# Second attention of a two-layer transformer kernel: two pairs on the two 64-row halves of the TensorE array, blocks of 16 score units, and row maxima moved by DMA

## What is computed

```python
Q = x @ wq + bq
K = x @ wk + bk
V = x @ wv + bv
Q = Q.reshape(B * H, S, D)      # B 4, H 16, S 1024, D 16: a plain reshape
K = K.reshape(B * H, S, D)
V = V.reshape(B * H, S, D)
scores = jnp.einsum('bqd,bkd->bqk', Q, K) / jnp.sqrt(jnp.float32(D))
attn = jax.nn.softmax(scores, axis=-1)
ctx = jnp.einsum('bqk,bkd->bqd', attn, V)
out = ctx.reshape(B, S, E) @ wo + bo + x      # and a layer norm
```

## Time and profile before

| | |
|---|---|
| median of 3 runs | 3050.78 us (3047.48 to 3051.34) |
| profiled execution, first to last instruction (span) | 3044.3 us |
| its own time | shown only as this span; what lies around it is in the runs' times |
| mean granted clock of TensorE | 0.896 |
| busy: PE / PE weight loads / DVE / ACT / POOL | 82% / 53% / 56% / 34% / 20% |

### The profile page before, as it was taken

How to read it: one execution, slowest core, us unless ns; L and a number is a source line. 1 busy time by engine, 2 the same in 40 slices (tenths; PEclk the granted TensorE clock), 3 DMA queues, 4 the chain that set the end, 5 groups by cost and what they waited for, 6 DMA issues and landing times. The chain is left out here.

```text
span 3044.3 us, 48668 instructions
## 1 busy us (share of the span) xinstructions
PE 2508.6 (82%) x15530; PEld 1604.6 (53%) x15531; DVE 1692.8 (56%) x2646; ACT 1020.5 (34%) x1877; POOL 602.4 (20%) x493
## 2 busy tenths in 40 slices
PE   3999999744889999999796859999999999945151
PEld 2777777642765555555585725545455455415041
DVE  3776777540333333333464457777777777537852
ACT  2444444210220000000222306666666666632010
POOL 4122121017000000000244311111111111120034
PEclk9999999756899999999898959999999999975566
DMA  5000000234421111110334893456364464011034
GB/s 194 2 0 0 0 0 0 83 141 171 160 83 33 34 36 35 34 34 31 118 114 144 241 114 28 29 39 46 29 46 39 35 50 28 1 59 56 0 105 144
DMA packets 213482, 193.01 MB, mean 63 GB/s; under 512 B 112810, under 2 KB 189266, under 8 KB 211314
## 3 DMA queue, kind: packets, MB, share of 16 engines
q1 hardware_dynamic: 198386, 140.07, 25.8%
q0 software_dynamic: 12672, 34.62, 3.7%
q10 hardware_dynamic: 2304, 16.78, 1.5%
HBM read 109.62 MB, written 81.79 MB: 63 GB/s over the span
## 5 line engine op out<-in xcount | busy, mean ns | idle before, releaser
L1621 DVE TENSOR_REDUCE a_nmax<-banks 128x1 f32<-128x1024 f32 x512 | 602.3, 1218 | 184.2 <-PE banks L1703 184.0
L1678 ACT ACTIVATE ga_probT<-banks 128x512 f32<-128x512 f32 x1024 | 555.9, 595 | 353.8 <-PE banks L1733 350.9
L1733 PE MATMUL banks<-a_qs,a_ks 128*128 128x512 f32 x1024 | 370.8, 439 | 17.9 <-ACT ga_probT L1678 8.7
L1703 PE MATMUL banks<-a_ks,a_qs 96*128 96x512 f32 x1024 | 309.8, 422 | 37.1 <-DMA ga_wo<-in_L_attn_wo_dram 27.4
L1654 POOL TENSOR_TENSOR a_qs<-ga_max_rows,a_tile_rows 32x1024 fp32r<-32x1024 f32 x64 | 151.4, 2365 | 758.7 <-DVE ga_max_rows L1627 758.7
L1733 PEld LDWEIGHTS banks<-a_qs,a_ks 128*128 128x128 f32 x1024 | 180.2, 193 | 210.3 <-ACT ga_probT L1678 178.7
L1179 PE MATMUL banks<-m_w,rb_xT 128*128 x576 | 288.9, 624 | 0.0
L1746 PE MATMUL banks<-ga_probT,a_v 128*32 128x512 f32 x2048 | 274.6, 608 | 0.9 <-ACT ga_probT L1678 0.9
L1026 PE MATMUL banks<-sh_xnT,sh_w 128*128 128x512 f32 x768 | 194.4, 409 | 81.0 <-issue 29.3
L1703 PEld LDWEIGHTS banks<-a_ks,a_qs 96*128 96x128 f32 x1024 | 192.0, 198 | 114.7 <-DVE a_nmax L1621 34.4
L1161 ACT ACTIVATE rb_silu<-banks 128x512 f32<-128x512 f32 x72 | 43.0, 597 | 516.1 <-PE banks L1179 516.1
(11 more groups left out here) (295 smaller groups left out, 3639.5 us busy)
## 6 DMA issues: line engine op xcount, KB each, us to landing
sh_xnT<-xnT_parts ACTq DMA_DIRECT2D x16, 1024.0 KB, 4.8
sorted_rows<-wa_zero SPq DMA_DIRECT2D x1, 9216.0 KB, 28.9
rb_xb<-sorted_rows POOLq DMA_DIRECT2D x72, 128.0 KB, 2.3
sorted_out<-rb_yb SPq DMA_DIRECT2D x72, 128.0 KB, 1.7
xnT_parts<-np_parts SPq DMA_DIRECT2D x8, 1024.0 KB, 4.5
m_w<-in_L_ffn_rw_dram SPq DMA_DIRECT2D x2, 4096.0 KB
values<-pg_v SPq DMA_DIRECT2D x16, 512.0 KB, 2.7
a_qs<-queries_rounded SPq DMA_DIRECT2D x32, 256.0 KB, 8.2
```

The costliest lines, as they stand in the source:

```text
L1621: nc.vector.tensor_reduce(nmax[:, gr, ST + q:ST + q + 1], slot[:], axis=AX.X, op=ALU.max, negate=True).then_inc(use_read, 1)
L1678: nc.scalar.activation(probT[(NS * pc + k) % SETS][n][:], b_t[h % 2][:], ACT.Exp, scale=SCALE).then_inc(exp_ready, 1)
L1703: last = nc.tensor.matmul(slot[:, HALF * hf:HALF * (hf + 1)], qs[a][0:ST, gr, P * q:P * (q + 1)], ks[a][0:ST, gr, HALF * hf:HALF * (hf + 1 ...
L1733: nc.tensor.matmul(b_t[h % 2][:], ks[a][:, n, P * k:P * (k + 1)], qs[a][:, n, HALF * hf:HALF * (hf + 1)], start=True, stop=True).then_inc( ...
```

## The change

Two pairs form a super, and there are eight. A pair's stacks now take 48 rows without gaps (three parts of 16), at row 0 for the first pair and at row 64 for the second; row 48 of each half is the row for the maxima in Q, with ones in K. Score products run over 48 rows, transposed ones over 49, each on a 64-row half of the array. A block is 16 score units: two pairs in turn, two groups, half of the queries. In a step PE issues a score product on one half, a transposed product of a block before on the other, and the same once more; the back half lags 22 units. The transposed products have three banks instead of two, `b_o` one instead of two, so that outputs are copied per block. Maxima are transposed once a block, and four DMAs from POOL write them to the rows at 48 and 112. The Fori loops of `group_attention` are gone: its steps are written out. `project_groups` loads the first super instead of the first pair, after waiting for both pairs' stores, and has fewer memsets.

```diff
+QK_IN, V_IN = 16 * 12, 16 * 2
+def load_super(eng, c, q_stack, k_stack, v, parts, values, qk_in, v_in):
+    for h in range(2):
+        for tile, n, blocks in ((q_stack, 0, (0, 0, 1)), (k_stack, 1, (0, 1, 0))):
+            for b, part in enumerate(blocks):
+                at = HR * h + DH * b
+                src = parts[n][part][2 * c + h].rearrange("(c d) (n t) -> d n c t", d=DH, n=NG)
+                eng.dma_start(tile[at:at + DH].bitcast(F32).rearrange("p n (c t) -> p n c t", c=PC), src).then_inc(qk_in, 16)
+        eng.dma_start(v[:, h].rearrange("p n q r -> p (n q r)"), values[2 * c + h]).then_inc(v_in, 16)
...
-            sp.wait_ge(parts_out[0], ONE + PARTS)
-            sp.wait_ge(v_out[0], ONE + 16)
-            load_pair(sp, 0, qs[0], ks[0], v_first, parts, values, first_in, first_in)
+            for s in range(2):
+                sp.wait_ge(parts_out[s], ONE + PARTS)
+                sp.wait_ge(v_out[s], ONE + 16)
+            load_super(sp, 0, qs[0], ks[0], v[0], parts, values, first_in, first_in)
...
-                nc.gpsimd.memset(ks[a][:].bitcast(F32), 0.0).then_inc(k_zero, 1)
...
-                nc.gpsimd.memset(qs[a][0:ST].bitcast(F32), 0.0).then_inc(stack_zero, 1)
...
+    HALF = L // 2
+    HQ = QT // 2
+    SUPERS = NP // 2
+    UB = 2 * 2 * HQ
+    BLOCKS = 4 * SUPERS
+    UNITS = UB * BLOCKS
+    LAG = UB + 6
+    SETS = 3
+    RING = 3
+    RB = UB // 2
...
+    def step_uses(s):
+        uses = [("scores", s)] if s < UNITS else []
+        if s % UB == 1 and UB < s < UNITS + UB:
+            uses.append(("maxima", s // UB - 1))
+        b, j = (s - LAG) // UB - 1, (s - LAG) % UB
+        if 0 <= b < BLOCKS and j == 3:
+            uses.append(("context", b))
+        if 0 <= b < BLOCKS and b % 2:
+            uses += [("contextT", b // 2)] * (j == 6) + [("project", b - 1)] * (j == 9) + [("project", b)] * (j == 11)
...
+            for b in range(BLOCKS):
...
+                pool.wait_ge(use_read, ONE + use_place["maxima", b] + 1)
+                for h in range(2):
+                    at = HR * h + ST
+                    for n in range(2):
+                        first = UB // 2 * h + HQ * n
+                        src = max_rows[b % 2][first:first + HQ].bitcast(F32)
+                        dst = q_cols[at:at + 1, 2 * gp + n].rearrange("o (q p) -> o q p", p=P)
+                        pool.dma_start(dst, src).then_inc(max_in[b % 2], 16)
...
+            def outputs(b):
+                act.wait_ge(pv_done, ONE + RB * (b + 1))
+                if b >= 2:
+                    act.wait_ge(use_done, ONE + use_place["context", b - 2] + 1)
+                nc.scalar.activation(o[b % 2][:], b_o[:], ACT.Copy).then_inc(o_ready, 1)
...
+            def scores(s, kh):
...
+                a, rows = c % SLOTS, slice(HR * h, HR * h + ST)
...
+            def scores_T(back, n):
...
+                a, h, kt = c % SLOTS, 1 - j % 2, j // 2
+                rows = slice(HR * h, HR * h + ST + 1)
+                if j == 0 and n == 0:
+                    pe.wait_ge(max_in[b % 2], 64 * (b // 2 + 1))
+                if w >= RING:
+                    pe.wait_ge(exp_ready, ONE + w - RING + 1)
+                nc.tensor.matmul(b_t[w % RING][:], ks[a][rows, 2 * gp + n, P * kt:P * (kt + 1)],
+                                 qs[a][rows, 2 * gp + n, HALF * hf:HALF * (hf + 1)], start=True, stop=True).then_inc(sT_done, 1)
...
+            for s in range(STEPS):
+                back = s - LAG
+                if s < UNITS:
...
+                    slot_of(use_place["scores", s])
+                    scores(s, 0)
+                if 0 <= back < UNITS:
+                    scores_T(back, 0)
+                if s < UNITS:
+                    scores(s, 1).then_inc(use_done, 1)
+                if 0 <= back < UNITS:
+                    scores_T(back, 1)
+                if back >= 2 and back % 2 == 0 and back <= UNITS:
+                    weigh(back // 2 - 1)
+                for kind, arg in step_uses(s):
+                    if kind != "scores":
+                        other[kind](arg)
```

More of the change, by code:

```diff
@@ L1506, in _, with group_attention @@
                 project(STEPS - 1, s)
[L1509 removed]
+def group_attention(nc, g, parts, values, qs, ks, v):
     ins = g.ins
[L1522 to L1555 removed]
@@ L1604, in _ @@
-            with sp.Fori(0, NP // SLOTS - 1) as r:
-                for c in range(SLOTS, 2 * SLOTS):
-                    load(r, c)
-            for c in range(NP // SLOTS * SLOTS, NP):
-                load(0, c)
+            for c in range(1, SUPERS):
+                a = c % SLOTS
+                if c >= SLOTS:
+                    sp.wait_ge(sT_done, ONE + 8 * UB * (c - SLOTS + 1))
+                    sp.wait_ge(pv_done, ONE + 4 * RB * (c - SLOTS + 1))
+                load_super(sp, c, qs[a], ks[a], v[a], parts, values, qk_in[a], v_in[a])
@@ L1687, in _, with weights @@
-            steps(act, step)
+            def weights(back, n):
+                w, k = 2 * back + n, back // 2
+                h = 1 - back % 2
+                act.wait_ge(sT_done, ONE + w + 1)
+                if back % 2 == 0 and n == 0 and k >= SETS:
+                    act.wait_ge(pv_done, ONE + k - SETS + 1)
+                nc.scalar.activation(probT[k % SETS][2 * h + n][:], b_t[w % RING][:], ACT.Exp, scale=SCALE).then_inc(exp_ready, 1)
+            def outputs(b):
[3 more added lines that the diff above has]
+                nc.scalar.activation(o[b % 2][:], b_o[:], ACT.Copy).then_inc(o_ready, 1)
@@ new lines, in maxima, with context @@
+            def maxima(b):
+                slot = slot_of(use_place["maxima", b])
+                pe.wait_ge(use_read, ONE + use_place["scores", UB * (b + 1) - 1] + 1)
+                nc.tensor.transpose(slot[:, 0:P], nmax[b % 2][:], g.ident[:]).then_inc(use_done, 1)
+            def context(b):
+                slot = slot_of(use_place["context", b])
+                pe.wait_ge(o_ready, ONE + b + 1)
+                for q in range(HQ):
+                    last = nc.tensor.transpose(slot[:, P * q:P * (q + 1)], o[b % 2][:, P * q:P * (q + 1)], g.ident[:])
+                last.then_inc(use_done, 1)
@@ new lines, in context_T, with project @@
+            def context_T(m):
+                slot = slot_of(use_place["contextT", m])
+                pe.wait_ge(use_read, ONE + use_place["context", 2 * m + 1] + 1)
+                for n in range(NG):
+                    last = nc.tensor.transpose(slot[:, P * n:P * (n + 1)], ctxn[:, n].rearrange("p q d -> p (q d)"), g.ident[:])
+                last.then_inc(use_done, 1)
+            def project(b):
+                slot = slot_of(use_place["project", b])
+                pe.wait_ge(use_read, ONE + use_place["contextT", b // 2] + 1)
+                h = b % 2
+                for a in range(A):
+                    last = nc.tensor.matmul(slot[:, 0:D], ctxT[:, h, a].rearrange("p n t -> p (n t)"), wo[:, a, :],
+                                            start=(a == 0), stop=(a == A - 1))
+                last.then_inc(use_done, 1)
@@ new lines, in _ @@
+            other = {"maxima": maxima, "context": context, "contextT": context_T, "project": project}
+            pe.wait_ge(w_in, ONE + 16 * QT)
+            for s in range(STEPS):
+                back = s - LAG
+                if s < UNITS:
+                    c = s // (4 * UB)
+                    if s % (4 * UB) == 0 and c > 0:
+                        pe.wait_ge(qk_in[c % SLOTS], ONE + QK_IN * (c // SLOTS + (c % SLOTS > 0)))
+                    slot_of(use_place["scores", s])
[8 more added lines that the diff above has]
+                    weigh(back // 2 - 1)
+                for kind, arg in step_uses(s):
+                    if kind != "scores":
+                        other[kind](arg)
```

311 lines of the change are left out of this document (99 added, 212 removed).

## The result

The changed kernel takes 3064.9 us (median of 12 runs, 3042.4 to 3078.6) against 3051.2 us for the kernel before, measured beside it (3034.8 to 3060.7): ratio 1.0039, 95% interval 1.0021 to 1.0057. It is slower by 0.4%. The forecast was 2935 us with a range of 2880 to 3046, so size and sign were wrong.

What follows compares the result with a forecast made beforehand. PE was taken to bound the kernel before, 98% busy in the joint stretch. Attention of 797 us plus 20 ahead, against 932.9, gave -116: span 2928, plus 6.5 for the runs' median, 2935 us; range 2880 to 3046.

Steps and rivals of the forecast that it cites:

- ahead of the attention: In project_groups, seven more loads on SP's queue before the last stores: 15 to 23 us, taken as 20.
- front: Start of the attention, only scores formed and reduced: 22 units at 1.378 us, 30.3 us.
- X: Time of one unit while both halves run: 1.712 us before, 1.48 forecast, own range 1.37 to 1.56.
- drain and tail: End of the attention after the last score product: 33 us for 22 units, plus 8.5 after the last weighing.
- Late by 0.55 us, taken as 0.6: Per block, PE's first transposed product waits for the maxima's POOL DMAs; bounds zero to some 5 us.
- twice the size at half the frequency and two supers of lead: no cost: Loads of the later supers during the attention were claimed to add no time.
- Maxima late: Rival: maxima DMAs land in 8 to 9 us instead of 4.75; 3055 us, or 2998 beside bursts only; chance 0.08.
- The clock: Rival: PE idling in the joint stretch brings 1.2 GHz, X 2.5; gain gone at a quarter of it; chance 0.04.
- The overlap of the halves: Score and transposed products on different row halves run at once, a pair in 0.233 us; chance 0.62.
- The loop through ACT: Products, two exponentials, then the weighing in PE's order: 2.71 us per two units, asking for X of 1.36.
- the rivals in which PE sets the pace: Own weights (3009 us, chance 0.12), no overlap (3046, 0.07), each change of half empties the array (3330, 0.07).
- Maxima and projections that stand in odd steps fall into its wait: In the joint stretch, this extra work was claimed to hide in the wait of ACT's loop.

Runs made afterwards that it cites:

- run 1: The changed kernel with the loads of supers 1 to 7 cut into small groups, each issued after a block's maxima have landed: 2891.05 us, ratio 0.9799.
- run 8: The changed kernel with all score and transposed products on one row half, so nothing runs side by side: 3433.94 us.
- run 3: The changed kernel with each weighing one step later, and output copy, context and projections later too: 2929.32 us, ratio 0.9921.
- run 4: The changed kernel with loads in small groups and the weighing one step later, both together: ratio 0.9685, and 0.9655 measured again.
- runs 9 and 10: On top of run 4, in odd steps the weighing ahead of the whole second pair (ratio 1.0222), or ahead of only the last transposed product (0.9762).

## Why the prediction was wrong

The miss is 3071.9 - 2928 = 144 us of span. Term by term:

| term | forecast | measured | miss |
|---|---|---|---|
| ahead of the attention | 20 | 25.7 | 6 |
| front | 30.3 | 35.2 | 5 |
| joint, bursts of loads | no cost | 71 | 71 |
| joint, X without that (0.6 a block for late maxima is in the forecast) | 1.48 | 1.575 | 47 |
| drain and tail | 41.5 | 55.6 | 14 |
| behind it | | | 1 |

**The maxima's DMAs: the step that failed.** The prediction had them "Late by 0.55 us, taken as 0.6", in every block, and of the loads it said "twice the size at half the frequency and two supers of lead: no cost". With no burst running the first was on the safe side: issue to landing is 1.6 us in the median where 2.3 was taken, and no wait is seen, so the 18 us set aside for it (0.6 a block) were free for the miss in X. The second was wrong. Fourteen loads in one burst hold SP's queue for 36 to 41 us, longer than a block, so a set of maxima always falls in it. Its last DMA then lands 9.1 to 13.9 us after issue. The rival "Maxima late" named that, at a chance of 0.08 and 63 us for blocks beside loads, and was turned down since "loads queue on SP's queue, the maxima don't". That the issuing queues are different was true and did not help: the maxima's packets stood for 6 us before the first was taken up, at a DMA share of 1.42 in the stall. Its price was near, 71 us in the joint stretch, but by luck: it took the mean DMA share of 0.52 for the part of the blocks that stand beside bursts, some 16 at 3.8 us, where six waits of 7.9 to 9.4 us (51 us) and the low clock around them make it up. The one bound that was written down, a landing of 6 to 7 us, was too low by half, though the row beside it had 14.7 for the loads themselves.

**The clock.** The rival stood at 0.04 as a case of its own. It came instead with the stalls: in each of the six of the joint stretch the level falls to 1.2 GHz while PE stands, and stays there for 10 to 24 us, of which 5 to 19 lie after the work is back. With the stalls gone (run 1) the stretch has 1.00. PE's waits on the maxima sum to 56.6 us, 5.3 of them at the end of the front, so 51 of the 71 us are waits; the other 20 are what else went with the stalls, the low clock behind them first of all. No run took the one without the other.

**X.** The overlap of the halves, the step with most at stake, was right: pairs at 0.23, starts 0.01 us apart or less, and 0.23 us a unit lost without it (run 8). The loop through ACT was right too: 2.71 per two units was forecast, 2.67 is what undisturbed ones take, and none of the rivals in which PE sets the pace came about. Wrong was the sentence "Maxima and projections that stand in odd steps fall into its wait". The timeline of an odd step with the maxima's transpose:

```profile
2226.24 1.06 PE L1696 MATMUL banks<-ga_probT,a_v 128*32 128x512 f32 x8
...
2227.90 0.33 PE L1703 MATMUL banks<-ident,ga_nmax 128*128 128x128 f32 x1
2228.00 1.22 DVE L1607 TENSOR_REDUCE ga_nmax<-banks 128x1 f32<-128x1024 f32 x1 [0.32 <-PE banks L1668]
2229.14 0.27 DVE L1612 CAST ga_max_rows<-banks 16x128 fp32r<-16x128 f32 x1
2229.28 0.50 PE L1668 MATMUL banks<-a_ks,a_qs 48*128 48x512 f32 x1 [1.05 <-DVE ga_nmax L1607]
...
2229.94 1.07 PE L1696 MATMUL banks<-ga_probT,a_v 128*32 128x512 f32 x8
```

From weighing to weighing 3.70 instead of 2.67. The transpose takes one of the two slots, so the next score product waits 1.05 us until the reduction of the unit just before ends; and the transposed products and the weighing stand behind it in PE's order. The prediction had this hand-over, priced at 0.4 us and on DVE only, where it would have hidden. In 32 units there are four such steps of +1.04, one of +2.10 with two extras, one of +0.59, and two of +0.49 for the copy of the outputs: 7.8 us, where the per-block allowance and the margin left 47.4 - 43.4 = 4.0 on the loop's 2.71. 16 x 2.67 + 7.8 = 50.5, the measured pair of blocks. Of this run 3 gives 2.2 back. The rest of the account is read off the timeline; no run tested the extras one by one. DVE, forecast as the bound at 88%, never was: it is 76% busy in the changed kernel, 83% with the stalls gone, 86% in run 4.

**Drain.** Forecast 33 us for 22 units, at full clock, since the old one "kept its clock". The new one fell to 0.50 and took 46.2 (2678.2 to 2724.4). In run 4 the level stayed at 1.00 until after the last weighing, and from the last score product to it took 34.0 us, nearly the forecast. Why the level fell in the one and held in the other is not shown: the weighing's place changes what PE does in it, and in the second measurement of run 4 it did fall, 27 us into the drain, which took 38.5.

**Ahead and front.** The first load holds SP's queue for 38.5 us instead of 15.1, 23.4 more: just over the bounds of 15 to 23. The first seven took 16.3 us and the second seven 22.2. Front: 29.1 us in run 1 (1721.6 to 1750.7), against 30.3 forecast; in the changed kernel block 0's maxima are caught as well, by the load of super 1, a wait of 5.3 us.

**The rule on weight loads** that a rival drew on (the Trainium skill, TensorE: Matmul & The Clock Gate, "The mechanism") did not bite. Within a step both score products use the same half, and in the rows of 2563.58 the load for the second runs under the first; the third pair follows after 0.23 us, where a load of 0.19 and a product of 0.23 in turn would take 0.42. In run 8, with all loads and products on the same rows, they follow each other at 0.23 as well. The rule of the Trainium skill (TensorEngine Tiling (Array Packing), "Key Properties") that changing the tile does not drain the array agrees: the pairs of two halves follow each other at 0.23, the pace at which full products streamed in the earlier trace rows.

## What to carry to other kernels

A wait that was moved from an engine to a DMA had here the latency of the worst moment, not of the quiet one: before putting a small transfer on the path, lay it beside the longest burst of any queue, and either spread the burst (one wait per group of loads, 71 us here) or give the transfer the burst's delay as lead (six units of lag). When the full engine is to be relieved (here of a quarter of its time by the forecast, 2.49 for 3.42 us), price the loops that were hidden under it: an extra use of a two-slot ring cost 1.04 us here where it stood in the step of the weighing, not the 0.33 of its instruction. And an order of products in a step belongs to two loops at once; what opens one (the banks behind ACT) can close the other (the slots behind DVE), as runs 9 and 10 show.

## What the runs showed of the hardware

Small DMAs issued on POOL's queue, with no burst running, land in the median 1.6 us after issue; beside a burst of loads on SP's queue, the same ones take 8 to 13.9 us, and their packets start late rather than run long. That they were issued on another queue did not spare them this.

Products on 48 rows of one half, one at a time, left the granted clock at 0.50 for 413 us with PE busy for 99%, and at other times ran at 1.00 with PE busy for 91 to 95% (run 8), while products in pairs on both halves had 1.00 over the joint stretch at 90% (run 1). In the joint stretch of the changed kernel each stall of 7.9 to 9.4 us came with 10 to 24 us at 0.50, 5 to 19 of them with the work back. What decides between the two levels the runs don't show.
